# Half or all of a state-space layer's output product moved from VectorE to TensorE and ScalarE, in the units that have no expert tile

## The chip, the cores and the metric

The kernel runs on one NeuronCore of one Trainium2 chip. The metric is the time of one execution on the device in microseconds (us). Several executions are timed and their median is taken; one further execution is recorded by the hardware profiler.

## What is computed

A batch of 2 sequences of 2048 tokens with 128 features goes through a pre-norm block: a Mamba layer, a gated feed-forward layer, and a mixture of 8 experts of which every token uses 2. The change touches the Mamba layer's recurrence. Cut to that:

```python
x_dbl = xc @ x_proj_w.T
dt, Bm, Cm = jnp.split(x_dbl, [DT_RANK, DT_RANK + D_STATE], axis=-1)      # 16 states
delta = jax.nn.softplus(dt @ dt_w.T + dt_b)
dA  = jnp.exp(jnp.einsum('bld,dn->bldn', delta, -jnp.exp(A_log)))
dBu = jnp.einsum('bld,bln,bld->bldn', delta, Bm, xc)
def step(h, inp):
    dA_t, dBu_t, C_t = inp
    h = dA_t * h + dBu_t                          # the scan over tokens
    y = jnp.einsum('bdn,bn->bd', h, C_t)          # multiply by C, sum over the 16 states
    return (h, y)
y = (ys + xc * D) * jax.nn.silu(z)
return y @ out_w.T                                # then feed-forward, routing, experts
```

## The kernel before

The 4096 tokens are cut into 8 chunks of 512. The recurrence of a chunk is done in 16 *units*, one for each state n. A unit handles 256 inner channels (two halves of 128 partitions) by 512 tokens. A unit takes these steps, named as in the code:

- `fetch_b`, `fetch_c`: SyncE starts DMAs that spread one row of B and one row of C over 128 partitions (`b_wide`, `c_wide`).
- `inflow` (GpSimd, L670): `du` times `b_wide`, 128x1024.
- `decay` (ScalarE, L775): two exponentials of 128x512, one for each half, into two PSUM banks. The one for unit i+1 waits for the scan of unit i on the same half.
- `scan` (VectorE, L908): two scans of 128x512 into `state`, which has two slots. Scan i waits for `inflow` i, `decay` i and the release of its slot.
- `carry` (ScalarE, L779): saves the last column for the next chunk.
- `times_c` (VectorE, L916): `state` times `c_wide`, one product of 128x1024 into `product`, two slots.
- `total` (TensorE, L1104): eight 128x128 transposes of `product`, which add up in the PSUM banks `y0` and `y1` over the 16 units of the chunk.
- After unit 15 of a chunk `y_gate` (VectorE, L924) reads `y0` and `y1`. It stands in VectorE's order after the scan of unit 0 of the next chunk.

Between these steps stands other work, placed by the function `plan()`: in unit n of chunk c one row of the table `FRONT` (norm, convolution, projections, softplus of chunk c+1) and one row of `BACK` (output projection, feed-forward and routing of chunk c-1). From chunk 3 on, most units also hold one expert tile of 128 rows (`x_turn`, `gate`, `up`, `moe_h`, `down`, `y_rows`), which uses the PSUM banks `gate` and `up`. All engines walk the same list `order`, each taking its own steps, so that a waiting step holds up all that stands behind it on its engine. The units hold 38 of the 78 expert tiles; the other 40 come after the last unit ("the tail").

Steps of `FRONT` and `BACK` that matter below: at n=4 `conv1` and `tanh_c`; at n=5 `xc` (VectorE, L879) and `x_proj` (TensorE, L1068); at n=6 `n_turn`, `n_t`, `ff_gate` (L1134) and `x_dbl`; at n=7 `gate_h` (ScalarE, L802 and L803) and `ff_val` (L1137); at n=8 `ff_out` (L1140, L1142); at n=9 `x_four` (VectorE, L943) and `log_dt`, whose logarithm needs two loads of ScalarE's tables; at n=12 `m_turn` (L1038) and `route_mm` (L1151); at n=13 `z0` (L1087); at n=14 `rank` (L1158 to L1163) and `z1`.

## Time and profile before

| | before |
|---|---|
| median of 3 runs | 914.85 us (913.28 to 917.78) |
| the profiled execution, its own time | 916.48 us |
| its span in the trace | 914.6 us |
| mean granted TensorE clock | 0.789 of 2.4 GHz |
| busy: VectorE, TensorE, GpSimd, ScalarE | 84%, 69%, 63%, 49% of the span |

The profile is of one execution. Its own time is 1.9 us longer than its span and 1.6 us above the median. PE is TensorE, DVE is VectorE, ACT is ScalarE, POOL is GpSimd, and L908 is line 908 of the kernel before.

### The profile page before, as it was taken

Reading aid. Unit: us, or ns where it says so; the run is one execution under the profiler, and the core shown is the slowest. Engines: PE = TensorE matmul, PEld = TensorE weight load, DVE = VectorE, ACT = ScalarE, POOL = GpSimd, SP = SyncE. Lnnn points to the kernel's source line nnn. Section 1 sums busy time; section 2 is a strip of 40 time slices with the busy share of each in tenths; the row PEclk is TensorE's granted clock in tenths of the full one; section 3 lists DMA queues with packets and bytes.
Section 4 is the critical chain, followed back from the end, with each engine's and each line's share of the span. In section 5 each row is a group of like instructions: output and inputs, shape, how many; then the busy total and the mean of one; then the engine's idle time right before and its main releaser. Section 6 shows DMA issues by size and latency. Waiting matters only on the chain.

```text
span 914.6 us, 12461 instructions
## 1 busy us (share of the span) xinstructions
PE 634.4 (69%) x3482; PEld 488.9 (53%) x3482; DVE 766.2 (84%) x1158; ACT 447.8 (49%) x924; POOL 577.8 (63%) x488
## 2 busy tenths in 40 slices
PE   4357377478757785797589658865884686887874
PEld 1134354365346435684477337743773475777863
DVE  1389899999989989989999999999999996363453
ACT  2446455644654475545555564647553352333421
POOL 1096376458746995789668976898589845235422
PEclk9577578758656966997699768977796679799987
DMA  6734233333323346533553355335543553446694
GB/s 175 244 104 142 91 116 100 120 94 121 124 76 96 118 117 169 161 113 99 175 161 107 96 185 151 127 93 161 172 120 113 149 145 94 125 140 191 185 308 132
DMA packets 99767, 126.06 MB, mean 138 GB/s; under 512 B 11831, under 2 KB 63875, under 8 KB 99683
## 3 DMA queue, kind: packets, MB, share of 16 engines
q1 hardware_dynamic: 95155, 115.89, 42.7%
q0 software_dynamic: 4544, 9.38, 2.8%
q8 instruction: 29, 0.48, 0.2%
q14 instruction: 39, 0.32, 0.1%
HBM read 113.23 MB, written 16.34 MB: 142 GB/s over the span
## 4 chain that ended last, share of the span: by engine, by line
DVE 35%; PE 29%; issue 18%; ACT 7%; DMA 4%; SPq 3%; POOL 3%; DVEq 1%; another core or an unknown queue 0%; POOLq 0%; ACTq 0%
DVE state L908 19%; DVE product L916 4%; PE work_front L1062 4%; PE y L1104 3%; PE gate L1181 3%; PE work_front L1068 3%; PE up L1188 3%; PE up L1199 2%; DVE stats L841 2%; PE work_front L1076 1%; DVE silu_m L1027 1%; PE work_side L1142 1%; DMA y_dram<-y_rows,x_rows 1%; DVE x_tok L945 1%; DVE conv L882 1%
## 5 line engine op out<-in xcount | busy, mean ns | idle before, releaser
L670 POOL TENSOR_TENSOR inflow<-du,b_wide 128x1024 f32<-128x1024 f32 x128 | 308.9, 2416 | 191.6 <-DVE product L916 153.8
L775 ACT ACTIVATE decay<-delta,a_neg 128x512 f32<-128x512 f32 x256 | 174.0, 689 | 199.4 <-DVE state L908 191.5
L1104 PE MATMUL y<-ident,product 128*128 128x128 f32 x1024 | 181.8, 337 | 119.9 <-DVE product L916 119.9
L1104 PEld LDWEIGHTS y<-ident,product 128*128 128x128 f32 x1024 | 153.5, 177 | 172.9 <-DVE product L916 138.3
L908 DVE TENSOR_TENSOR_SCAN state<-decay,carry,inflow 128x512 f32<-128x512 f32 x192 | 235.2, 1266 | 0.8 <-ACT decay L775 0.8
L916 DVE TENSOR_TENSOR product<-state,c_wide 128x1024 f32<-128x1024 f32 x128 | 189.5, 1480 | 1.3
L697 POOL DMA_INDIRECT y_dram<-y_rows,x_rows x78 | 87.5, 1121 | 90.5 <-ACT y_rows L831 82.4
L691 POOL DMA_INDIRECT row_dram<-m_tok,place x64 | 71.8, 1122 | 22.1 <-issue 12.8
L908 DVE TENSOR_TENSOR_SCAN state<-decay,inflow 128x512 f32<-128x512 f32 x64 | 74.5, 1205 | 7.0 <-ACT decay L775 4.5
L1062 PE MATMUL work_front<-u_t,w_tap 128*128 128x512 f32 x128 | 63.0, 618 | 4.0 <-ACT u_t L725 1.7
L1181 PE MATMUL gate<-x_cols,w_stage 128*128 128x128 f32 x306 | 50.5, 309 | 7.4 <-ACT x_cols L821 6.9
L1199 PE MATMUL up<-w_down,h_cols 128*128 (+1 forms) x306 | 47.9, 296 | 8.8 <-DVE h_cols L1032 5.4
L1188 PE MATMUL up<-x_cols,w_stage 128*128 128x128 f32 x306 | 49.6, 304 | 5.3 <-ACT y_rows L831 3.3
L1181 PEld LDWEIGHTS gate<-x_cols,w_stage 128*128 128x128 f32 x306 | 44.5, 218 | 10.3 <-ACT x_cols L821 9.5
L1199 PEld LDWEIGHTS up<-w_down,h_cols 128*128 128x128 f32 (+1 forms) x306 | 41.1, 204 | 14.0 <-issue 14.0
L1188 PEld LDWEIGHTS up<-x_cols,w_stage 128*128 128x128 f32 x306 | 43.8, 216 | 6.3 <-ACT y_rows L831 4.1
L1068 PE MATMUL work_front<-xc,w_xproj 128*40 128x512 f32 x32 | 26.5, 978 | 27.5 <-DVE xc L879 27.5
L831 ACT ACTIVATE y_rows<-up,x_rows 128x128 f32<-128x128 f32 x51 | 18.7, 368 | 45.0 <-PE up L1199 37.6
L826 ACT ACTIVATE tanh_m<-gate 128x384 f32<-128x384 f32 x51 | 25.1, 492 | 30.7 <-PE gate L1181 23.4
L1087 PE MATMUL work_front<-w_in,u_t 128*128 128x256 f32 x64 | 24.2, 517 | 18.5 <-DVE silu_z L899 17.7
L1062 PEld LDWEIGHTS work_front<-u_t,w_tap 128*128 128x128 f32 x128 | 22.9, 198 | 24.8 <-issue 17.7
L1027 DVE SCALAR_TENSOR_TENSOR silu_m<-tanh_m,gate 128x384 f32<-128x384 f32 x51 | 27.4, 536 | 9.9 <-ACT tanh_m L826 7.1
(199 smaller groups left out, 1118.4 us busy)
## 6 DMA issues: line engine op xcount, KB each, us to landing
b_wide<-bc_dram SPq DMA_DIRECT2D x128, 256.0 KB
c_wide<-bc_dram SPq DMA_DIRECT2D x128, 256.0 KB
w_stage<-gate_up_dram SPq DMA_DIRECT2D x78, 344.0 KB
x_rows<-row_dram SPq DMA_DIRECT2D x78, 65.0 KB
x_tok<-in_x SPq DMA_DIRECT2D x8, 256.0 KB, 6.0
out<-x_tok SPq DMA_DIRECT2D x8, 256.0 KB
inflow<-y_dram SPq DMA_DIRECT2D x6, 256.0 KB, 4.8
gate_up_dram<-in_Wg SPq DMA_DIRECT2D x1, 1376.0 KB, 9.1
```

What stands on the lines that cost most here:

```text
L670: e.tensor_tensor(inflow[:, key % 3], du[:, c % 2], b_wide[:, key % ROW_SLOTS:key % ROW_SLOTS + 1, :].to_broadcast([P, HALVES, CHUNK]), AL ...
L691: e.indirect_dma_start(row_dram, bass.IndirectOffsetOnAxis(place[:, c, q, s:s + 1], 0), m_tok[:, c % M_SLOTS, s, :], None).then_inc(S[f"d_ ...
L697: e.indirect_dma_start(y_dram, bass.IndirectOffsetOnAxis(x_rows[:, key % X_SLOTS, ID_AT:ROW].bitcast(u32), 0), y_rows[:, key % Y_SLOTS, :] ...
L775: e.activation(decay_bank[h][:], delta[:, c % 2, h, :], ACT.Exp, scale=a_neg[:, h, n:n + 1]).then_inc(S["decay"], 1)
L908: e.tensor_tensor_scan(state[:, key % STATE_SLOTS, h, :], decay_bank[h][:], inflow[:, key % 3, h, :], 0.0 if c % (SEQ // CHUNK) == 0 else ...
L916: e.tensor_tensor(product[:, key % 2], state[:, key % STATE_SLOTS], c_wide[:, key % ROW_SLOTS:key % ROW_SLOTS + 1, :].to_broadcast([P, HAL ...
L1062: t = e.matmul(front[:], w_tap[:, k, h * P:(h + 1) * P], u_t[:, key % 2, k:k + CHUNK], start=k == 0, stop=k == D_CONV - 1)
L1068: t = e.matmul(front[0:BC + DT_RANK, :], w_xproj[:, h, :], xc[:, key % 2, h, :], start=h == 0, stop=h == HALVES - 1)
L1104: t = e.matmul(y_bank[s // 2][:, y_at(s, h)], product[:, key % 2, h, s * P:(s + 1) * P], ident[:], is_transpose=True, start=False, stop=n ...
L1181: t = e.matmul(gate[:, q * P:(q + 1) * P], w_stage[:, key % W_SLOTS, 0, q * P:(q + 1) * P], x_cols[:, key % 2, :], start=True, stop=True)
L1188: t = e.matmul(up[:, q * P:(q + 1) * P], w_stage[:, key % W_SLOTS, 1, q * P:(q + 1) * P], x_cols[:, key % 2, :], start=True, stop=True)
L1199: t = e.matmul(up[:, FF_WIDE:], h_cols[:n, key % 2, q, :], w_down[:n, bass.ds(experts[j % PICKS], 1), q, :].rearrange("p o d -> p (o d)"), ...
```

## The change

In units that have no expert tile (`free` in `plan()`, 46 of 128) C is applied by another way. The state itself is turned by TensorE into the idle banks `gate` and `up` (`h_turn`), so that tokens lie on partitions. There C is one number for each partition, and ScalarE copies the bank to SBUF with C as its scale (`c_scale`, into `h_rows`, one slot). TensorE then adds it to `y0` and `y1` by a product with the identity (`total`). In n=10 to 15 all four blocks of 128 tokens go this way, and VectorE's product and its C row are left out: 23 *full* units (six in each of chunks 0, 1 and 2, and n=10 in chunks 3 to 7). In n=4, 5 and 6 two of the four blocks do, and VectorE's product is 128x2x256: 23 *half* units (n=4 of chunk 4 is not among them). C turned for this is made once a chunk by four small products (`c_turn`) and one copy (`c_rows`). `inflow`, `scan` and `x_turn` get the waits that the new readers ask for, and `z0` now waits for `c_rows`. In the diff, `c_scale` is on ScalarE, `times_c` on VectorE, `total` and `h_turn` on TensorE.

```diff
+SHARES = {4: 2, 5: 2, 6: 2, 10: SUB, 11: SUB, 12: SUB, 13: SUB, 14: SUB, 15: SUB}
...
             turn(m, i)
+        if i in shares:
+            put("h_turn", i)
+            put("c_scale", i)
         put_all(back[1], front[1])
...
+        if not moving and ("x_turn", m) not in done and n in SHARES:
+            free.append(i)
         put("times_c", i)
...
+                elif name == "c_scale":
+                    c, n = UNITS[key]
+                    e.wait_ge(S["h_turn"], turned[key])
+                    e.wait_ge(S["y_sum"], key)
+                    e.wait_ge(S["c_rows"], c + 1)
+                    for sub in range(SUB - share[key], SUB):
+                        e.activation(h_rows[:, sub, :], h_bank[sub // 2][:, sub % 2 * D_INNER:(sub % 2 + 1) * D_INNER], ACT.Copy,
+                                     scale=c_tok[:, c % 2, sub, n:n + 1]).then_inc(S["c_scaled"], 1)
...
                 elif name == "times_c":
-                    c, n = UNITS[key]
+                    if share[key] == SUB:
+                        continue
+                    wide = (SUB - share[key]) * P
...
-                    e.tensor_tensor(product[:, key % 2], state[:, key % STATE_SLOTS],
-                                    c_wide[:, key % ROW_SLOTS:key % ROW_SLOTS + 1, :].to_broadcast([P, HALVES, CHUNK]), ALU.mult).then_inc(S["times_c"], 1)
+                    e.tensor_tensor(product[:, key % 2, :, :wide], state[:, key % STATE_SLOTS, :, :wide],
+                                    c_wide[:, key % ROW_SLOTS:key % ROW_SLOTS + 1, :wide].to_broadcast([P, HALVES, wide]), ALU.mult).then_inc(S["times_c"], 1)
...
                 elif name == "total":
-                    e.wait_ge(S["times_c"], key + 1)
-                    for s in range(SUB):
+                    alone = SUB - share[key]
+                    if alone:
+                        e.wait_ge(S["times_c"], products[key])
+                    for s in range(alone):
                         for h in range(HALVES):
                             t = e.matmul(y_bank[s // 2][:, y_at(s, h)], product[:, key % 2, h, s * P:(s + 1) * P], ident[:],
                                          is_transpose=True, start=False, stop=n == D_STATE - 1, skip_group_check=True)
+                    if share[key]:
+                        e.wait_ge(S["c_scaled"], scaled[key])
+                    for r in range(alone // 2, 2):
+                        t = e.matmul(y_bank[r][:], ident[:], h_rows[:, 2 * r:2 * r + 2, :].rearrange("p s d -> p (s d)"), start=False, stop=n == D_STATE - 1,
+                                     skip_group_check=True)
                     t.then_inc(S["y_sum"], 1)
+                elif name == "h_turn":
+                    e.wait_ge(S["scan"], HALVES * (key + 1))
+                    if scaled[key] > share[key]:
+                        e.wait_ge(S["c_scaled"], scaled[key] - share[key])
+                    if tiles_ahead[key]:
+                        e.wait_ge(S["y_rows"], tiles_ahead[key])
+                    for s in range(SUB - share[key], SUB):
+                        for h in range(HALVES):
+                            t = e.transpose(h_bank[s // 2][:, y_at(s, h)], state[:, key % STATE_SLOTS, h, s * P:(s + 1) * P], ident[:])
+                    t.then_inc(S["h_turn"], 1)
```

TensorE's order from the `total` of n=11 to that of n=14 in chunk 2. Before (`y<-ident,product` at L1104 is a `total`):

```order
L1104 MATMUL y<-ident,product 128x128 x32
L1038 MATMUL work_side<-ident,m_tok 128x128 x4
L1151 MATMUL work_side<-w_route,n_t 128x8 x4
L1104 MATMUL y<-ident,product 128x128 x8
L1087 MATMUL work_front<-w_in,u_t 128x256 x2
L1104 MATMUL y<-ident,product 128x128 x8
```

And of the change, from the `total` of n=11 to that of n=13 (L1172 is `h_turn`, L1156 the product of the identity with `h_rows` in `total`):

```order
L1156 MATMUL y<-h_rows,ident 128x512 x2
L1083 MATMUL work_side<-ident,m_tok 128x128 x4
L1172 MATMUL gate<-ident,state 128x128 x4
L1172 MATMUL up<-ident,state 128x128 x4
L1218 MATMUL work_side<-w_route,n_t 128x8 x4
L1156 MATMUL y<-h_rows,ident 128x512 x2
L1172 MATMUL gate<-ident,state 128x128 x4
L1172 MATMUL up<-ident,state 128x128 x4
L1132 MATMUL work_front<-w_in,u_t 128x256 x2
L1156 MATMUL y<-h_rows,ident 128x512 x2
```

In a full unit TensorE now has two steps in place of one, and the `total` of a unit stands ahead of the `h_turn` of the next.

TensorE's order from `x_proj` at n=5 to the `total` of n=6 in chunk 2, before:

```order
L1068 MATMUL work_front<-xc,w_xproj 40x512 x2
L1104 MATMUL y<-ident,product 128x128 x8
L1038 MATMUL work_side<-ident,m_tok 128x128 x4
L1134 MATMUL work_side<-n_t,w_ffg 128x512
L1076 MATMUL work_front<-x_dbl,w_dt 128x512
L1104 MATMUL y<-ident,product 128x128 x8
```

And of the change:

```order
L1113 MATMUL work_front<-xc,w_xproj 40x512 x2
L1151 MATMUL y<-ident,product 128x128 x4
L1156 MATMUL y<-h_rows,ident 128x512
L1083 MATMUL work_side<-ident,m_tok 128x128 x4
L1172 MATMUL up<-ident,state 128x128 x4
L1201 MATMUL work_side<-n_t,w_ffg 128x512
L1121 MATMUL work_front<-x_dbl,w_dt 128x512
L1151 MATMUL y<-ident,product 128x128 x4
L1156 MATMUL y<-h_rows,ident 128x512
```

The `h_turn` of n=6 now stands between `n_turn` (L1083) and `ff_gate` (L1201). On ScalarE the `c_scale` of the same unit now stands ahead of `n_t` (L837), for which `ff_gate` waits:

```order
L815 ACTIVATE decay<-delta,a_neg 128x512 x2
L819 ACTIVATE carry<-state 128x2
L780 ACTIVATE h_rows<-up,c_tok 128x256 x2
L837 ACTIVATE n_t<-work_side,norm_gb 128x512
L768 ACTIVATE x_dbl<-work_front 40x512
```

Before, `n_t` followed `carry` directly.

## Rows read from the trace of the kernel before

**Rows 1.** The page: busy time and share of the span of each engine.
```profile
PE 634.4 (69%) x3482; PEld 488.9 (53%) x3482; DVE 766.2 (84%) x1158; ACT 447.8 (49%) x924; POOL 577.8 (63%) x488
```

**Rows 2.** The page: costliest groups; busy us, mean ns, idle before and its releaser.
```profile
L775 ACT ACTIVATE decay<-delta,a_neg 128x512 f32<-128x512 f32 x256 | 174.0, 689 | 199.4 <-DVE state L908 191.5
L1104 PE MATMUL y<-ident,product 128*128 128x128 f32 x1024 | 181.8, 337 | 119.9 <-DVE product L916 119.9
L916 DVE TENSOR_TENSOR product<-state,c_wide 128x1024 f32<-128x1024 f32 x128 | 189.5, 1480 | 1.3
```

**Rows 3.** Timeline, VectorE, chunk 0, n=10 to `y_gate`: start, us, instruction.
```profile
95.59 2.34 DVE L908 TENSOR_TENSOR_SCAN state<-decay,inflow 128x512 f32<-128x512 f32 x2 [4.31 <-ACT decay L775]
...
126.56 1.27 DVE L924 TENSOR_TENSOR y_gated<-silu_z,y 128x512 f32<-128x512 f32 x2
```

**Rows 4.** Timeline, VectorE, chunk 1, n=10 to `y_gate`.
```profile
171.24 2.46 DVE L908 TENSOR_TENSOR_SCAN state<-decay,carry,inflow 128x512 f32<-128x512 f32 x2 [0.84 <-ACT decay L775]
...
186.39 1.21 DVE L916 TENSOR_TENSOR product<-state,c_wide 128x1024 f32<-128x1024 f32 x1
187.52 2.45 DVE L908 TENSOR_TENSOR_SCAN state<-decay,carry,inflow 128x512 f32<-128x512 f32 x2
...
207.57 1.26 DVE L924 TENSOR_TENSOR y_gated<-silu_z,y 128x512 f32<-128x512 f32 x2
```

**Rows 5.** Timeline, all engines: TensorE, ScalarE and VectorE at work like the new steps.
```profile
202.70 1.29 ACT L775 ACTIVATE decay<-delta,a_neg 128x512 f32<-128x512 f32 x2
203.47 0.68 DVE L899 SCALAR_TENSOR_TENSOR silu_z<-silu_z,work_front 128x512 f32<-128x512 f32 x1
207.02 1.11 PE L1038 MATMUL work_front<-ident,u_tok 128*128 128x128 f32 x4 [0.58 <-ACT u_tok L719]
208.41 0.76 ACT L725 ACTIVATE u_t<-work_front,norm_gb 128x512 f32<-128x512 f32 x1
213.41 1.04 PE L1104 MATMUL y<-ident,product 128*128 128x128 f32 x8
214.72 1.88 PE L1062 MATMUL work_front<-u_t,w_tap 128*128 128x512 f32 x4
229.74 1.97 PE L1104 MATMUL y<-ident,product 128*128 128x128 f32 x8 [3.23 <-DVE product L916]
234.43 3.54 PE L1068 MATMUL work_front<-xc,w_xproj 128*40 128x512 f32 x4 [2.73 <-DVE xc L879]
```

**Rows 6.** The groups by line, ScalarE: a copy with a scale, and one without.
```profile
L831 ACT ACTIVATE y_rows<-up,x_rows 128x128 f32<-128x128 f32 x51 | 18.7, 368 | 45.0 <-PE up L1199 37.6 <-remote 6.3 <-issue 1.1
...
L813 ACT ACTIVATE n_t<-work_side 128x512 f32<-128x512 f32 x8 | 4.7, 585 | 0.9 <-issue 0.9
```

**Rows 7.** Timeline, TensorE, the other steps of n=12 to 14 in chunk 1.
```profile
184.68 1.06 PE L1038 MATMUL work_side<-ident,m_tok 128*128 128x128 f32 x4
186.62 1.87 PE L1151 MATMUL work_side<-w_route,n_t 128*128 128x8 f32 x8 [0.88 <-ACT n_t L813]
...
196.68 0.63 PE L1158 MATMUL work_side<-both,before 128*128 128x32 f32 x2 [0.93 <-DVE both L980]
...
200.12 2.05 PE L1087 MATMUL work_front<-w_in,u_t 128*128 128x256 f32 x4
```

**Rows 8.** Windows: busy us of PE, PEld, DVE, ACT, POOL; granted clock, DMA.
```profile
95.00:127.00 32.00, 14.90 (x60) 11.95 (x60) 31.23 (x37) 14.96 (x33) 17.11 (x12) 0.55 0.25 81
171.00:208.00 37.00, 22.77 (x95) 18.96 (x93) 36.27 (x64) 16.83 (x39) 21.27 (x16) 0.55 0.29 92
258.00:295.00 37.00, 22.78 (x96) 19.55 (x96) 36.52 (x65) 15.82 (x36) 23.07 (x16) 0.55 0.29 92
127.00:171.00 44.00, 32.96 (x159) 20.00 (x158) 43.02 (x54) 28.89 (x49) 25.62 (x13) 0.89 0.38 128
```

**Rows 9.** Timelines, VectorE and TensorE: `x_four` at n=9 of chunks 3, 5; `ff_out`.
```profile
342.66 0.69 DVE L943 TENSOR_TENSOR x_two<-x_two,work_side 128x512 f32<-128x512 f32 x1 [3.25 <-PE work_side L1142]
...
532.62 0.67 DVE L943 TENSOR_TENSOR x_two<-x_two,work_side 128x512 f32<-128x512 f32 x1
...
530.45 1.16 PE L1142 MATMUL work_side<-w_ffp,gate_h 128*128 128x128 f32 x8
```

**Rows 10.** Timeline, VectorE and GpSimd: one product beside an `inflow`.
```profile
422.92 3.46 DVE L916 TENSOR_TENSOR product<-state,c_wide 128x1024 f32<-128x1024 f32 x1
422.92 2.37 POOL L670 TENSOR_TENSOR inflow<-du,b_wide 128x1024 f32<-128x1024 f32 x1
```

More of the change, by code:

```diff
@@ L76 @@
     ((), ("pre_dt1",), ("exp_dt",)),
-    (("log_dt",), (), ()),
-    ((), ("series", "small", "log1p"), ()),
+    (("log_dt",), (), ("c_turn",)),
+    ((), ("c_rows", "series", "small", "log1p"), ()),
     ((), ("delta",), ()),
@@ L113 @@
 HEAD = ["stats0", "rstd0", "rstd1", "shift0", "x_one", "prepare", "u_tok", "u_turn", "u_t", "halo", "in0a", "in0b", "conv0", "in1a", "in1b",
-        "conv1", "tanh_c", "xc", "x_proj", "x_dbl", "dt0", "pre_dt0", "dt1", "pre_dt1", "exp_dt", "log_dt", "series", "small", "log1p",
+        "conv1", "tanh_c", "xc", "x_proj", "x_dbl", "dt0", "pre_dt0", "dt1", "pre_dt1", "exp_dt", "log_dt", "c_turn", "c_rows", "series", "small", "log1p",
         "delta", "du"]
@@ L313, in plan @@
         put(step, last)
-    return order, tail
+    if not shares:
+        return plan(free)
+    return order, shares, tail
 def mamba_moe_block(nc, T, out):
@@ L445, in mamba_moe_block @@
             + ["dt", "pre_dt", "exp_dt", "log_dt", "ser0", "series", "small", "log1p", "delta", "du", "z", "tanh_z", "silu_z"]
-            + ["inflow", "decay", "scan", "carry", "times_c", "y_skip", "y_sum", "y_gate", "y_turn", "y_cols"]
+            + ["inflow", "decay", "scan", "carry", "times_c", "c_turn", "c_rows", "h_turn", "c_scaled", "y_skip", "y_sum", "y_gate", "y_turn", "y_cols"]
             + ["out_proj", "x_two", "n_tok", "n_turn", "n_t", "ff_gate", "gate_evac", "ff_val", "silu_g", "ff_h", "ff_out"]
@@ L668, in _ @@
                     if key >= 3:
-                        e.wait_ge(S["times_c"], key - 2)
+                        if share[key - 3] < SUB:
+                            e.wait_ge(S["times_c"], products[key - 3])
+                        else:
+                            e.wait_ge(S["scan"], HALVES * (key - 2))
                     e.tensor_tensor(inflow[:, key % 3], du[:, c % 2], b_wide[:, key % ROW_SLOTS:key % ROW_SLOTS + 1, :].to_broadcast([P, HALVES, CHUNK]),
@@ L1081, in _ @@
                     else:
[L1082 removed]
+                        e.wait_ge(S["c_rows"], key + 1)
                     if not key:
```

42 lines of the change are left out of this document (35 added, 7 removed).

## Prediction

> **What bounds the kernel now.** I read the page first. VectorE is busy for 84% of the span, TensorE for 69%, ScalarE for 49% [rows 1]. In the groups of the page the `decay` of ScalarE, the `total` of TensorE and, by its releaser column, most other work of the units wait for VectorE's scan or product, while the product itself hardly waits (1.3 us for 128) [rows 2]. So inside the units VectorE sets the pace, and a product of 1.2 us taken out of its queue should bring that much nearer the end, as long as nothing else becomes the last to arrive. That condition is the whole question, so I read VectorE's timeline next, in the three stretches where full units stand one behind the other: n=10 to 15 of chunks 0, 1 and 2. From the scan of n=10 to `y_gate`, the first instruction that needs the sums of all 16 units, 31.0 us pass in chunk 0 (95.59 to 126.56) [rows 3] and 36.3 us in chunk 1 (171.24 to 207.57) [rows 4]. In chunk 2, which repeats chunk 1, I take the same. VectorE is busy for 31.2 of 32 and 36.3 of 37 us there. TensorE has little to do and its granted clock is 0.55, so nearly all is at the lower level, 1.2 GHz. In the stretch between (127 to 171) it was 0.89 [rows 8]. A product takes a slot of 1.13 us in VectorE's order (186.39 to 187.52) [rows 4]. The last 40 expert tiles come after the units and the change does not touch them.
>
> **The new steps in a full unit.** No row shows them, so each is built from its nearest.
> - `h_turn`: eight 128x128 transposes, the same work as the old `total`: 1.04 us at the high clock, 1.97 at the low one [rows 5].
> - TensorE to ScalarE: the turn that ends at 208.13 releases `u_t` at 208.41, 0.28 us [rows 5].
> - `c_scale`: four copies of 128x256 from PSUM with a scale. A copy of 128x128 with a scale takes 0.368 [rows 6], a 128x512 with a scale 0.689 [rows 2], so 128x256 lies at 0.475. Two in a row overlap by 0.09 (2 x 0.689 less 1.29) [rows 5]. Four take 1.63 us.
> - `total`: two products of 128x512: 1.88 at the high clock, 3.54 at the low one [rows 5].
>
> These steps form a ring. `total` i waits for `c_scale` i, `c_scale` i for `h_turn` i, and `h_turn` i+1 stands behind `total` i on TensorE. There is one slot of `h_rows` and one pair of banks. So the ring cannot overlap with itself: a full unit cannot take less than 1.04 + 0.28 + 1.63 + 1.88 = **4.8 us** at the high clock and 1.97 + 0.28 + 1.63 + 3.54 = **7.4 us** at the low one. Behind a waiting `c_scale` on ScalarE stands the `decay` of unit i+2, and with it the scan, so VectorE is held to the ring after about one unit of lead. VectorE itself would need 36.3/6 less 1.13, about 4.9 us a unit in chunks 1 and 2, and 4.0 in chunk 0. The ring takes the product's place as the bound.
>
> Other steps of these units lie inside the ring in chunks 1 and 2, at the high clock (half the low-clock rows): `m_turn` 0.5; `m_t` and `route_mm`, which wait behind `c_scale` 12: 0.28 + 0.59 + 0.94 = 1.8 [rows 6, 7]; `rank` and `z1`, from 196.68 to 202.17 at the low clock, so 2.7, of which 1.9 lies beside `c_scale`: 0.8 [rows 7]. Sum 3.1 us; at the low clock 1.1 + 2.7 + 3.6 = 7.4.
>
> **Which clock.** The first full unit finds TensorE as idle as before: 7.4. In it TensorE works 5.5 of 7.4 us, more densely than before, and I expect the clock to rise during the second (6.1, the mean), and to stay up in the last four (4 x 4.8 = 19.2).
> - Chunk 0: 2.3 (scan) + 7.4 + 6.1 + 19.2 = 35.0 against 31.0: +4.0.
> - Chunks 1 and 2: 2.5 + 7.4 + 6.1 + 19.2 + 3.1 = 38.3 against 36.3: +2.0 each.
>
> Together **+8.0**. Bounds: all at the high clock, 31.1 and 34.4, so 0 and twice -1.9: -3.8. All at the low clock, 46.7 and 54.3, so +15.7 and twice +18.0: +51.7.
>
> The Trainium skill (TensorE: Matmul & The Clock Gate, Part 1) says that the low clock is the default and that activity releases it. By that rule alone, the added products would lift the clock in all of these stretches, and this term would be near its lower bound, -3.8. The trace agrees in direction (0.55 where TensorE is busy 15 of 32 us, 0.89 where it is busy 33 of 44) [rows 8], and not on whether a ring with gaps of 1.9 us is active enough.
>
> **Single full units** (n=10 of chunks 3 to 7). No second full unit follows, VectorE has three softplus steps there and ScalarE is free. The ring is hidden behind VectorE's n=10. The product's slot is gained: 5 x 1.13 = **-5.7**. If TensorE is late there, nothing is gained: 0.
>
> **Half units.** VectorE's half product is like a 128x512 (0.68 [rows 5] for 1.22): -0.54 each, -12.4 for all 23, if VectorE stays the last to arrive. A product that meets an `inflow` takes 3.46 us [rows 10], about one after the other; a half product meets it as well and saves no more. But at n=5 to 8 of chunks 1 to 7 there is a chain through TensorE: `xc`, `x_proj`, `total` 5, `n_turn`, `n_t`, `ff_gate`, `total` 6, `ff_val`, `ff_out`, `x_four`. In chunk 3 VectorE waits 3.25 us for its end [rows 9], and likewise in chunks 2, 4 and 7. Into this chain come, at the high clock: `total` 5 and `total` 6 each lose four transposes (0.52) and gain a product of 128x512 (0.94): +0.42 twice; `h_turn` 6: 0.52; `c_scale` 6 with its release, ahead of `n_t`: 0.28 + 0.86. Sum 2.5 (3.7 at the low clock). `xc` comes 0.5 earlier, which leaves +2.0 (3.2). So chunks 2, 3, 4 and 7: 4 x 2.0 = +8.0. In chunks 1, 5 and 6 VectorE doesn't wait, and comes about 1 us after the chain's end (531.6 against 532.6 in chunk 5) [rows 9]: 3 x 1.0 = +3.0. Chunk 0 has no such chain: 3 x -0.54 = -1.6. Sum **+9.4**. Bounds: -12.4 (the chain has room everywhere), and at the low clock 4 x 3.2 + 3 x 2.2 - 1.6 = +17.8.
>
> **The rest, at nothing.** `c_turn` and `c_rows`, once a chunk: four small products (like `route_mm`, 1.87 [rows 7]) and one copy of 128x64 (under 0.37 [rows 6]); they lie at n=9 and 10 beside VectorE's softplus steps, and `z0`, which waits for them, comes at n=13. Without that cover, 8 x 0.4 = 3 us on ScalarE. SyncE starts 23 C rows fewer; no B row is late now. ScalarE's own load, 138 copies of 0.41, fits into its idle half. The Trainium skill (ScalarE: Activation LUTs, Rules for kernel authors) advises VectorE for a multiplication. Here four copies take 1.63 us against one product of 1.22, so the move trades a shorter for a longer step and pays only where ScalarE is not in the chain.
>
> **Sum.** 8.0 + 9.4 - 5.7 = +11.7 us on the profiled execution's 916.5: 928.2. That execution is 1.6 above the median of 914.85, so **926.5 us** for the median.
>
> **The rivals.**
> - *The clock stays low in the rings.* For it: 0.55 now, and each `c_scale` leaves a gap. Against it: TensorE works for three quarters of a slow ring. All low gives 914.85 + 51.7 + 17.8 - 5.7 = 979; half of the way there from my value, about 953. Chance 0.15 for more than 940.
> - *The clock rises at once*, because the added products keep TensorE at work from the first full unit on. -3.8 + 9.4 - 5.7 = -0.1: 915, no difference. For it: 0.89 in the stretch in which TensorE has more work [rows 8]. Against it: the first full unit starts at the low clock. Chance 0.13. This is what the clock gate's rule of the Trainium skill, named above, would do here.
> - *VectorE stays the bound in the half units, so the kernel is faster.* Place: n=5 to 9. `h_turn` and `total` of n=4 and 5 give TensorE work just where it idles ahead of `x_proj`. If that keeps the clock up, `x_proj` alone takes 1.9 in place of 3.54 [rows 5], and two or three steps at the higher clock pay for the 2.0 us. It decides once the chain ends 2 us sooner in chunks 2, 3, 4 and 7. With the rings at the high clock: -3.8 - 12.4 - 5.7 = -21.9: 893; with my rings, 8.0 - 18.1 = -10.1: 905. For it: the chain ran at both clocks. Against it: `x_proj` would have to find the clock up although TensorE idles ahead of it, 2.73 us in chunk 2 [rows 5]. Chance 0.27.
> - *My forecast*, VectorE held by the rings and by the longer chain: 0.45, by itself 919.5 to 940.
>
> **How the numbers follow.** About 0.5% (4.6 us) is what a measurement of this kernel can tell from no change. Slower: 0.45 + 0.15 = 0.60. Within: 0.13. Faster: 0.27. The range leaves out about one in ten at each end: the best part of the faster case, below 900, and the worst part of the low clock, above 952.
>
> **What the profile after would show.** Right: in n=10 to 15 of chunks 0 to 2, the scans of VectorE are idle before, released by `decay`, and `decay` by `c_scale`; starts of `h_turn` 4.8 to 7.4 us apart; 35 and 38 us from the scan of n=10 to `y_gate`; longer waits of L988 (`x_four`) in chunks 2 and 3; four `c_scale` copies in 1.6 us. Wrong: scans back to back in these stretches; a granted clock near 1.0 there from the first full unit on; `x_four` without a wait. The forecast falls if one full unit's ring is much shorter than 4.8 us, or if the half units' chain ends before VectorE arrives.

## The result, and the profile after

| | before | changed |
|---|---|---|
| median | 918.35 us (913.28 to 927.35, 8 runs) | 907.12 us (905.76 to 913.85, 8 runs) |
| the profiled execution: its time, its span | 916.48, 914.6 us | 908.7, 906.5 us |
| mean granted TensorE clock | 0.789 | 0.870 |

The ratio is 0.990, with a 95% interval of 0.9861 to 0.9939: the changed kernel is faster by about 1%, some 9 us. Ratios and intervals here leave out executions more than 1.5% above the fastest of their kernel (before, the one at 927.35 us; of norings_late, the profiled one at 910.3 us), medians and ranges keep them. The forecast was slower, 926.5; the time lies in the range from 900 to 952, the sign was wrong.

The page of the changed kernel, busy line and groups (columns as in [rows 1, 2]):

```profile
PE 669.6 (74%) x3684; PEld 487.7 (54%) x3684; DVE 735.0 (81%) x1135; ACT 496.7 (55%) x1070; POOL 575.0 (63%) x488
...
L815 ACT ACTIVATE decay<-delta,a_neg 128x512 f32<-128x512 f32 x256 | 172.1, 690 | 113.6 <-DVE state L951 107.2
L961 DVE TENSOR_TENSOR product<-state,c_wide 128x1024 f32<-128x1024 f32 (+1 forms) x105 | 144.8, 1379 | 4.8 <-PE y L1151 3.4
...
L1156 PE MATMUL y<-h_rows,ident 128*128 128x512 f32 x138 | 90.2, 773 | 28.5 <-ACT h_rows L780 28.5
...
L780 ACT ACTIVATE h_rows<-up,c_tok 128x256 f32<-128x256 f32 x92 | 38.5, 474 | 14.8 <-PE up L1172 14.8
```

VectorE does 31 us less, and the kernel is 8 to 9 us shorter. So most of what VectorE was spared did not reach the end, and the questions are where it went and why anything was left. I looked at the three places that the prediction names.

**The full units of chunk 0**, TensorE's timeline of the changed kernel. L1172 is `h_turn`, L1156 `total`:

```profile
99.19 1.12 PE L1172 MATMUL gate<-ident,state 128*128 128x128 f32 x4 [5.23 <-DVE state L951]
100.10 1.06 PE L1172 MATMUL up<-ident,state 128*128 128x128 f32 x4
102.82 3.78 PE L1156 MATMUL y<-h_rows,ident 128*128 128x512 f32 x4 [1.66 <-ACT h_rows L780]
106.64 0.71 PE L1172 MATMUL gate<-ident,state 128*128 128x128 f32 x4
...
109.45 1.99 PE L1156 MATMUL y<-h_rows,ident 128*128 128x512 f32 x4 [1.66 <-ACT h_rows L780]
111.27 0.60 PE L1172 MATMUL gate<-ident,state 128*128 128x128 f32 x4
...
115.79 0.60 PE L1172 MATMUL gate<-ident,state 128*128 128x128 f32 x4
```

The ring is there. The first `h_turn` to the second takes 7.45 us at the low clock (predicted 7.4), from the second on 4.5 to 4.6 (predicted 6.1, then 4.8). In chunks 1 and 2, where other steps lie between, the starts are 7.6, 6.5, 5.9, 4.5 and 5.2 us apart, and 7.6, 5.0, 6.5, 5.4 and 5.2. Each wait of 1.66 us is four copies on ScalarE and the two hand-overs, of 0.03 to 0.06 us each. ScalarE's copies in the second ring of chunk 0, which begin when the turns end (107.79) and end 0.05 us before `total`:

```profile
107.83 0.84 ACT L780 ACTIVATE h_rows<-gate,c_tok 128x256 f32<-128x256 f32 x2 [0.39 <-PE up L1172]
108.56 0.84 ACT L780 ACTIVATE h_rows<-up,c_tok 128x256 f32<-128x256 f32 x2
```

Windows of the changed kernel (columns as in [rows 8]): the first ring of chunk 0, its other rings, n=10 to `y_gate` of chunks 1 and 2, and n=4 to 10 of chunks 2 and 3:

```profile
96.80:106.60 9.80, 5.75 (x12) 2.75 (x12) 9.66 (x8) 4.49 (x11) 3.15 (x1) 0.50 0.15 39
106.60:127.50 20.90, 14.31 (x65) 8.67 (x64) 16.40 (x23) 15.01 (x37) 15.90 (x11) 1.00 0.35 102
...
172.70:209.80 37.10, 26.24 (x109) 15.82 (x108) 31.81 (x58) 23.72 (x59) 24.13 (x18) 0.83 0.24 74
257.00:294.00 37.00, 26.54 (x108) 16.37 (x108) 33.90 (x57) 23.69 (x59) 23.74 (x18) 0.82 0.22 73
227.10:257.20 30.10, 22.15 (x99) 12.14 (x97) 28.11 (x33) 24.30 (x41) 20.90 (x12) 0.94 0.30 97
311.00:343.30 32.30, 22.24 (x88) 11.75 (x88) 31.44 (x34) 24.30 (x41) 27.29 (x27) 0.83 0.44 129
```

VectorE is now idle for 4.5 of 20.9 us in the rings, where it was busy for 31.2 of 32 [rows 8]. VectorE's timeline of the changed kernel gives the length of these stretches:

```profile
96.80 2.34 DVE L951 TENSOR_TENSOR_SCAN state<-decay,inflow 128x512 f32<-128x512 f32 x2 [4.32 <-ACT decay L815]
...
129.54 1.29 DVE L969 TENSOR_TENSOR y_gated<-silu_z,y 128x512 f32<-128x512 f32 x2 [2.93 <-PE y L1156]
...
172.74 2.46 DVE L951 TENSOR_TENSOR_SCAN state<-decay,carry,inflow 128x512 f32<-128x512 f32 x2 [1.54 <-ACT decay L815]
...
209.76 1.28 DVE L969 TENSOR_TENSOR y_gated<-silu_z,y 128x512 f32<-128x512 f32 x2 [1.03 <-PE y L1156]
```

Chunk 0: 32.7 us against 31.0 [rows 3] (predicted 35.0). Chunk 1: 37.0 against 36.3 [rows 4] (predicted 38.3). Chunk 2: 37.0 against 36.4. So the 18 products that left these stretches bought nothing: they became 3.0 us *longer*.

**The half units' chain**, chunk 2. First the kernel before, then the changed one: `xc`, `ff_out`, `x_four` (for `x_proj` before: [rows 5]).

```profile
233.17 1.21 DVE L879 SCALAR_TENSOR_TENSOR xc<-tanh_c,conv 128x1024 f32<-128x1024 f32 x1
...
252.42 2.08 PE L1142 MATMUL work_side<-w_ffp,gate_h 128*128 128x128 f32 x8
...
254.53 0.69 DVE L943 TENSOR_TENSOR x_two<-x_two,work_side 128x512 f32<-128x512 f32 x1 [3.46 <-PE work_side L1142]
```

```profile
234.19 1.21 DVE L919 SCALAR_TENSOR_TENSOR xc<-tanh_c,conv 128x1024 f32<-128x1024 f32 x1
...
235.45 1.91 PE L1113 MATMUL work_front<-xc,w_xproj 128*40 128x512 f32 x4 [1.68 <-DVE xc L919]
...
250.46 1.16 PE L1209 MATMUL work_side<-w_ffp,gate_h 128*128 128x128 f32 x8
...
251.69 0.66 DVE L988 TENSOR_TENSOR x_two<-x_two,work_side 128x512 f32<-128x512 f32 x1
```

From `xc` to `x_four` 21.4 us became 17.5, although TensorE has more to do between them. `x_proj` takes 1.91 in place of 3.54, `ff_out` 1.16 in place of 2.08, and `x_four` no longer waits. The granted clock of n=4 to 10 of this chunk is 0.94 [windows above], before it was 0.64. In chunk 3 `x_proj` still runs at the low clock (3.64 us), and the same distance falls all the same, from 21.0 to 17.9 us. The groups of `x_four`, of before and of the changed kernel, whose last columns are VectorE's idle time ahead of it:

```profile
L943 DVE TENSOR_TENSOR x_two<-x_two,work_side 128x512 f32<-128x512 f32 x8 | 5.4, 679 | 10.6 <-PE work_side L1142 10.6
```

```profile
L988 DVE TENSOR_TENSOR x_two<-x_two,work_side 128x512 f32<-128x512 f32 x8 | 5.3, 666 | 2.4 <-PE work_side L1209 2.4
```

The forecast had this wait grow by 2 us in each of four chunks. It shrank by 8.2 in all. The prediction also read it wrongly: it has a wait "likewise in chunks 2, 4 and 7", and before, these were 3.46, 0.81 and 0.66 us (3.25 in chunk 3). In chunks 4 and 7:

```profile
437.73 0.69 DVE L943 TENSOR_TENSOR x_two<-x_two,work_side 128x512 f32<-128x512 f32 x1 [0.81 <-PE work_side L1142]
...
721.72 0.69 DVE L943 TENSOR_TENSOR x_two<-x_two,work_side 128x512 f32<-128x512 f32 x1 [0.66 <-PE work_side L1142]
```

The remaining 2.38 us of both groups stand in the tail, behind the last unit, and stay.

**Something that the prediction did not have.** VectorE and GpSimd just behind the scan of n=10 in chunk 1, before:

```profile
174.93 0.69 DVE L886 TENSOR_SCALAR tanh_c<-tanh_c 128x1024 uint32<-128x1024 f32 x1
...
178.22 2.35 POOL L670 TENSOR_TENSOR inflow<-du,b_wide 128x1024 f32<-128x1024 f32 x1 [3.98 <-DVE product L916]
```

and in the changed kernel:

```profile
175.36 3.15 POOL L696 TENSOR_TENSOR inflow<-du,b_wide 128x1024 f32<-128x1024 f32 x1 [0.33 <-DVE state L951]
...
176.41 2.65 DVE L926 TENSOR_SCALAR tanh_c<-tanh_c 128x1024 uint32<-128x1024 f32 x1
```

Before, the `inflow` of n=13 waited for the product of n=10 (178.22). Now that there is no product, it waits for the scan (175.36), comes 3 us sooner, and meets the comparison of softplus (`small`). That takes 2.65 us in place of 0.69. Scan 10 to scan 11 grew from 6.7 to 7.6 us, although a product of 1.13 is gone. In chunks 3 to 6 GpSimd still has two steps of a norm (`rstd`) to do there, this `inflow` starts only after the comparison has ended (at 348.65 in chunk 3, where the comparison starts at 347.06 and takes 0.69), and the same distance shrank by 1.07 to 1.35 us (in chunk 3 from 6.83 to 5.76). In chunk 7, without softplus steps, it shrank by 1.26.

### The profile page after: what moved, and what is told of

It reads as the page before. It is cut to its first block, busy times and chain, and to the rows that moved or that the text cites. A ratio compares the mean times of both kernels' runs of the same rounds, so it can differ in the third digit from the quotient of the medians.

```text
span 906.5 us, 13029 instructions
## 1 busy us (share of the span) xinstructions
PE 669.6 (74%) x3684; PEld 487.7 (54%) x3684; DVE 735.0 (81%) x1135; ACT 496.7 (55%) x1070; POOL 575.0 (63%) x488
## 4 chain that ended last, share of the span: by engine, by line
PE 25%; DVE 20%; issue 12%; ACT 6%; DMA 2%; SPq 2%; another core or an unknown queue 1%; POOL 0%; DVEq 0%; ACTq 0%; POOLq 0%
DVE state L951 10%; PE gate L1250 3%; PE up L1268 2%; DVE product L961 2%; PE up L1257 2%; PE y L1156 2%; PE y L1151 2%; PE work_front L1107 2%; PE work_front L1113 1%; ACT decay L815 1%; DVE stats L881 1%; DVE silu_m L1072 1%; DVE x_tok L990 1%; PE decay L1250 1%
## 5 line engine op out<-in xcount | busy, mean ns | idle before, releaser
L696 POOL TENSOR_TENSOR inflow<-du,b_wide 128x1024 f32<-128x1024 f32 x128 | 317.3, 2482 | 177.5 <-DVE product L961 116.9
L815 ACT ACTIVATE decay<-delta,a_neg 128x512 f32<-128x512 f32 x256 | 172.1, 690 | 113.6 <-DVE state L951 107.2
L961 DVE TENSOR_TENSOR product<-state,c_wide 128x1024 f32<-128x1024 f32 (+1 forms) x105 | 144.8, 1379 | 4.8 <-PE y L1151 3.4
L1151 PE MATMUL y<-ident,product 128*128 128x128 f32 x748 | 111.7, 294 | 42.5 <-DVE product L961 42.5
L1151 PEld LDWEIGHTS y<-ident,product 128*128 128x128 f32 x748 | 91.9, 152 | 80.4 <-DVE product L961 50.1
L1156 PE MATMUL y<-h_rows,ident 128*128 128x512 f32 x138 | 90.2, 773 | 28.5 <-ACT h_rows L780 28.5
L717 POOL DMA_INDIRECT row_dram<-m_tok,place x64 | 72.6, 1134 | 24.6 <-issue 14.6
L1107 PE MATMUL work_front<-u_t,w_tap 128*128 128x512 f32 x128 | 65.7, 641 | 6.0 <-ACT u_t L751 4.4
L1156 PEld LDWEIGHTS y<-h_rows,ident 128*128 128x128 f32 x138 | 28.9, 239 | 51.6 <-ACT h_rows L780 35.5
L1257 PE MATMUL up<-x_cols,w_stage 128*128 128x128 f32 x306 | 47.6, 295 | 6.9 <-ACT y_rows L871 6.9
L780 ACT ACTIVATE h_rows<-up,c_tok 128x256 f32<-128x256 f32 x92 | 38.5, 474 | 14.8 <-PE up L1172 14.8
```

Source lines behind the costliest of these rows:

```text
L696: e.tensor_tensor(inflow[:, key % 3], du[:, c % 2], b_wide[:, key % ROW_SLOTS:key % ROW_SLOTS + 1, :].to_broadcast([P, HALVES, CHUNK]), AL ...
L717: e.indirect_dma_start(row_dram, bass.IndirectOffsetOnAxis(place[:, c, q, s:s + 1], 0), m_tok[:, c % M_SLOTS, s, :], None).then_inc(S[f"d_ ...
L815: e.activation(decay_bank[h][:], delta[:, c % 2, h, :], ACT.Exp, scale=a_neg[:, h, n:n + 1]).then_inc(S["decay"], 1)
L961: e.tensor_tensor(product[:, key % 2, :, :wide], state[:, key % STATE_SLOTS, :, :wide], c_wide[:, key % ROW_SLOTS:key % ROW_SLOTS + 1, :wi ...
L1107: t = e.matmul(front[:], w_tap[:, k, h * P:(h + 1) * P], u_t[:, key % 2, k:k + CHUNK], start=k == 0, stop=k == D_CONV - 1)
L1151: t = e.matmul(y_bank[s // 2][:, y_at(s, h)], product[:, key % 2, h, s * P:(s + 1) * P], ident[:], is_transpose=True, start=False, stop=n ...
```

## The experiments

One table for all: the ratio to the kernel before, run beside each on the same chip, and from the one profile of each three sums over VectorE's timeline, from the start of one scan to that of another: (a) n=10 to n=1 of the next chunk, chunks 0 to 2; (b) the same, chunks 3 to 6; (c) n=4 to n=10, all eight chunks, with the granted clock there.

| | median | ratio, 95% interval | a | b | c, clock |
|---|---|---|---|---|---|
| before | | | 111.8 | 170.7 | 258.8, 0.74 |
| copy | 916.15 | 0.9986 (0.9957 to 1.0015) | 111.7 | 173.1 | 256.1, 0.74 |
| changed kernel | 907.12 | 0.9900 (0.9861 to 0.9939) | 113.9 | 165.4 | 248.9, 0.89 |
| halves | 912.39 | 0.9931 (0.9903 to 0.9960) | 111.7 | 175.4 | 249.1, 0.88 |
| fulls | 908.34 | 0.9897 (0.9865 to 0.9929) | 113.4 | 165.6 | 249.8, 0.80 |
| warm | 912.11 | 0.9932 (0.9906 to 0.9958) | 111.7 | 172.5 | 250.0, 0.86 |
| half_product | 908.36 | 0.9890 (0.9841 to 0.9939) | 111.6 | 173.0 | 244.0, 0.76 |
| no_c | 896.44 | 0.9767 (0.9733 to 0.9801) | 100.9 | 166.9 | 251.1, 0.80 |
| two_slots | 906.71 | 0.9887 (0.9851 to 0.9923) | 109.8 | 169.0 | 247.2, 0.86 |
| norings | 904.13 | 0.9857 (0.9824 to 0.9891) | 113.8 | 166.8 | 246.1, 0.86 |
| late_inflow | 906.46 | 0.9897 (0.9861 to 0.9933) | 111.3 | 165.3 | 248.5, 0.88 |
| warm_ring | 909.80 | 0.9908 (0.9872 to 0.9944) | 114.3 | 165.4 | 248.2, 0.88 |
| singles | 905.16 | 0.9862 (0.9818 to 0.9906) | 111.7 | 165.5 | 247.3, 0.85 |
| norings_late | 897.77 | 0.9783 (0.9744 to 0.9822) | 107.9 | 169.5 | 251.2, 0.85 |

Column a repeats to 0.2 us where nothing of it was changed (before, copy, halves, warm, half_product, singles). Columns b and c differ by more between executions in which nothing of them was changed (b by 2.4 us in copy and 4.7 in halves, c by 2.7 in copy), and the clock of single chunks differs with them, so they carry a verdict only together with the timed ratio.

### copy: the kernel before, once more

No edit. 

> The kernel before once more, unchanged but for an empty line, as a second profile of it and as a measure of what no change looks like. All theories: a ratio of 1 within its interval. It tells how far the stages n=0 to 4, 4 to 10 and 10 to 16 of single profiled executions differ without any change: the profile before had 258.8 us in n=4 to 10 over all chunks, and each of the four edited kernels 244 to 250. If the copy has 250 as well, that difference was the draw of one execution and no effect of the half units.

Measured: 0.9986, no difference. Its column c is 256.1 us, so of the 9.9 us that this column is shorter in the changed kernel, some 3 can be the draw of one execution, and not all. `x_four` waits as before, 11.7 us.

### halves and fulls: one part of the change at a time

```diff
-SHARES = {4: 2, 5: 2, 6: 2, 10: SUB, 11: SUB, 12: SUB, 13: SUB, 14: SUB, 15: SUB}
+SHARES = {4: 2, 5: 2, 6: 2}                                    # halves
+SHARES = {n: SUB for n in range(10, D_STATE)}                  # fulls
```

> The change with the 23 half units only; no unit is full. Theory A (the half units give the gain, because TensorE's added work keeps its clock up in n=4 to 10 and the chain from xc to x_four ends sooner; the full units together are worth little): 907 to 911 us against about 917 before, the granted clock of n=4 to 10 in chunks 2, 3 and 7 up by 0.1 or more against 0.64, 0.70 and 0.60. Theory B (my prediction's term: the half units cost 9 us, and the gain is in the full ones): 924 to 928 us. Theory C (the gain is from the full units' clock, which carries over into the other stages): about 917, no difference.

> The change with the 23 full units only; no unit is half. Theory A: the rings of chunks 0 to 2 cost about 3 us, the five single units gain 5.5, so 913 to 917 us. Theory B: 905 or less. Theory C: 907 to 910.

Measured: the half units alone gain 6.3 us, the full ones alone 9.5, both together 9.2. The half units' term of the forecast (+9.4) thus has the wrong sign. The gains don't add: whatever each of them gives, they partly give the same. The profiled execution of halves, at 920.2 us, is the slowest of its twelve. That full units gain 9.5 is more than the single ones in column b (5.1) less the 1.6 that column a costs. The time of fulls lies in the range of Theory C (907 to 910), a clock that carries over into other stages. The rest appears in column c, where fulls adds only `c_turn` (1.06 us of TensorE once a chunk) but the granted clock of chunks 2 and 3 is 0.83 and 0.83 after 0.64 and 0.70. How much of it is chance, a single profile can't say, and no run shows what carries the clock over.

### warm: TensorE's added work without VectorE's saving

The kernel before, with one 128x512 product of constants into the idle bank `up` behind the `total` in each of the 23 half units. Nobody reads it.

```diff
                     t.then_inc(S["y_sum"], 1)
+                    if key in tiles:
+                        if tiles[key]:
+                            e.wait_ge(S["y_rows"], tiles[key])
+                        e.matmul(up_bank[:], ident[:], w_in[:], start=True, stop=True)
```

> The kernel before with one more product of 128x512 on TensorE in each of the 23 half units, right behind the unit's total, of constants into the idle bank up, read by nobody; VectorE and ScalarE as before. The output is the reference's. It has TensorE's load of the half units without VectorE's saving. Theory A (clock): the granted clock of n=4 to 10 rises as in the changed kernel and the kernel is faster than before by 3 to 8 us. Rival (VectorE's shorter product gives the gain, TensorE's work only costs): the same as before or slower by up to 5 us.

Measured: 0.9932, 6.2 us faster by work that serves nothing. The group of `x_four`:

```profile
L946 DVE TENSOR_TENSOR x_two<-x_two,work_side 128x512 f32<-128x512 f32 x8 | 5.4, 672 | 3.1 <-PE work_side L1149 3.1
```

VectorE waits 3.1 us there in place of 10.6, and the granted clock of n=4 to 10 is 0.86 in place of 0.74. That the clock is higher is not the draw of one profile: over its twelve executions the mean granted clock is 0.808 to 0.824, against 0.776 to 0.796 for the kernel before. VectorE's load is unchanged, so here the clock shortens the chain.

### half_product: VectorE's saving without the added work

```diff
+                    wide = 2 * P if key in tiles else CHUNK
-                    e.tensor_tensor(product[:, key % 2], state[:, key % STATE_SLOTS], ...
+                    e.tensor_tensor(product[:, key % 2, :, :wide], state[:, key % STATE_SLOTS, :, :wide], ...
```

> The kernel before with VectorE's product cut to 128x2x256 in the 23 half units; TensorE turns the same eight blocks as before, half of them old data. Left out: half of the multiplication by C in these units. It has VectorE's saving without any work for TensorE or ScalarE. Theory A (clock): at most 3 us faster, since the chain's end at x_four still comes late at the low clock in chunks 2, 3, 4 and 7. Rival (the shorter product gives the gain): 8 to 12 us faster.

Measured: 0.9890, 10.1 us for 23 half products of 0.54 each (12.4). By the interval it is 5.6 to 14.6 us. VectorE is the bound in most of these units: much of what it is spared arrives at the end, at a mean clock of 0.76 in column c, hardly above the old one. My chain, which should have swallowed this, holds only where VectorE waits for it, and that was 8.2 us in all units together. How much is VectorE's saving alone, the run doesn't show. In its profile the granted clock of chunks 2 and 3 is 0.76 and 0.80 after 0.64 and 0.70, without added work, and `x_four` waits there no longer (in chunk 4 it waits 3.70); column c is shorter by 14.8 us, more than the 12.4 of the products. halves has this saving, the warmth of TensorE and the new steps, and gains 6.3. If the three simply added, the new steps in the chain would cost about 10 us (10.1 + 6.2 - 6.3). That sum is arithmetic, no run isolates it.

### no_c: full units without their ring

fulls, but the turned state goes straight into `y`: no `c_scale`, no product with the identity, one `total` of eight transposes.

```diff
-            put("c_scale", i)
...
+                        for s in range(SUB):
+                            for h in range(HALVES):
+                                t = e.matmul(y_bank[s // 2][:, y_at(s, h)], state[:, key % STATE_SLOTS, h, s * P:(s + 1) * P], ident[:],
+                                             is_transpose=True, start=False, stop=n == D_STATE - 1, skip_group_check=True)
```

> Full units only, without the ring: in the 23 full units VectorE's product is left out and TensorE's total turns the state straight into the sum; no h_turn, no c_scale, no identity product. Left out: the multiplication by C in these units. It shows what the 23 products are worth on VectorE. If the rings of chunks 0 to 2 hold VectorE as I predicted (h_turn starts 4.5 us apart), this kernel is 12 to 20 us faster than the one with the full units only (about 908), so 890 to 897. If the rings hold nothing, it is within 4 us of it.

Measured: 0.9767, 21.4 us, against 9.5 for fulls. The difference of 11.9 us is in column a: 100.9 against 113.4. So the detour (the separate turn, the copies, the products with the identity) costs 12.5 us in 18 units, and takes all that their products release (10.9 here, where the comparison still takes 2.65 us and scan 10 to 11 7.4 to 7.6). In chunk 0 TensorE does denser work than before, without a 128x512 product. Its window there, scan 11 to the scan behind n=15:

```profile
104.30:122.10 17.80, 10.72 (x48) 8.55 (x48) 17.77 (x25) 8.94 (x19) 14.05 (x11) 0.63 0.25 82
```

### two_slots: a ring that may overlap with itself

```diff
-        h_rows = sb("h_rows", [P, SUB, D_INNER])
+        h_rows = sb("h_rows", [P, 2, SUB, D_INNER])
...
+            if late:                       # n = 11 to 15: total i-1 behind h_turn i
+                put("total", i - 1)
```

> The changed kernel with a second slot of h_rows, and in n=11 to 15 of chunks 0 to 2 the total of a unit put behind the h_turn of the next, so that the identity products of one unit lie beside the c_scale of the next. If the ring holds VectorE: the starts of h_turn fall from 4.5 us apart to 3.4 to 4, n=10 to y_gate from about 33 and 37 us to 27 and 31, and the kernel is 8 to 15 us faster than the changed one (about 909). If it is VectorE's and ScalarE's own order that holds these units: within 3 us of it.

Measured: 0.9887, hardly better than the changed kernel. TensorE's timeline shows that the ring is broken open in chunk 0:

```profile
99.06 1.12 PE L1175 MATMUL gate<-ident,state 128*128 128x128 f32 x4 [3.66 <-DVE state L954]
...
106.48 1.12 PE L1175 MATMUL gate<-ident,state 128*128 128x128 f32 x4 [5.45 <-DVE state L954]
...
111.38 0.60 PE L1175 MATMUL gate<-ident,state 128*128 128x128 f32 x4
...
114.17 0.63 PE L1175 MATMUL gate<-ident,state 128*128 128x128 f32 x4
```

From the third on the starts are 2.8 to 3.9 us apart in place of 4.5, and chunk 0 takes 30.1 us from n=10 to `y_gate` (32.7 in the changed kernel, 27 expected). But the second turn (106.48) now waits for the scan, no longer for the ring, and still comes 7.4 us after the first: it is scan 11 that is late, behind softplus and its collision. In chunks 1 and 2, 38.5 and 38.8 us of column a (39.4 and 39.3 in the changed kernel) are left, so what the ring held there is 0.9 us and less a chunk, and other steps of n=11 to 15 come next.

### norings: full units without a neighbour

`SHARES = {4: 2, 5: 2, 6: 2, 10: SUB}`: n=10 stays full in all chunks, n=11 to 15 go back to VectorE. 

> The changed kernel without full units in n=11 to 15: half units, and n=10 full in all eight chunks. My theory now (a ring costs about what it saves, 1 to 2 us a chunk): within 4 us of the changed kernel, 905 to 912. Rival (the 15 full units behind n=10 carry the gain, by the clock that they keep up): slower than the changed kernel by 5 to 9 us.

Measured: 0.9857. That is within 4 us of the changed kernel, as expected, at 904.1 just below the expected 905. Column a is 113.8, that of the changed kernel. The 15 full units behind n=10 in chunks 0 to 2 are worth nothing: they trade their products for waits on the ring.

### late_inflow and norings_late: the collision taken away

```diff
                             e.wait_ge(S["scan"], HALVES * (key - 2))
+                    if n == 13 and c < 3:
+                        e.wait_ge(S["small"], c + 2)
```

> The changed kernel, with one wait more: in chunks 0 to 2 the inflow of n=13, which GpSimd computes, starts only after VectorE's softplus comparison (small, 128x1024). In the changed kernel this inflow waits for the scan of n=10 in place of a product, runs beside the comparison, and the comparison takes 2.65 us in place of 0.69. Theory H (this collision cancels the gain of n=10 in these chunks): the comparison takes 0.7 again, scan 10 to scan 11 falls from 7.4 to 7.6 us to about 5.7, and the kernel gains up to 3 x 1.9 = 5.7 us on the changed one: ratio to the kernel before 0.982 to 0.986, some 902 to 904. Theory R (the rings from n=10 on hold the stretch in any case): scan 10 to 11 falls, but the waits behind it grow by as much, n=10 to y_gate stays at 32.7 and 37.0 us within 0.5, and the time stays at 906 to 908, ratio 0.988 to 0.991.

> Half units, and n=10 full in all chunks, none behind it; and in chunks 0 to 2 the inflow of n=13 starts only after the softplus comparison, as in late_inflow. No ring can take back what the comparison gains. If the collision (2.65 us for 0.69) is what eats the gain of n=10 there, scan 10 to scan 11 of chunks 0 to 2 is about 5.7 us and the kernel is some 3 to 5 us faster than the one with n=10 full and no late inflow (0.9857): ratio 0.980 to 0.983, 900 to 902. If that inflow was hidden and something else is next in line, the ratio stays at 0.984 to 0.987.

GpSimd and VectorE of norings_late in chunk 1:

```profile
177.55 0.69 DVE L928 TENSOR_SCALAR tanh_c<-tanh_c 128x1024 uint32<-128x1024 f32 x1
...
178.41 3.38 POOL L698 TENSOR_TENSOR inflow<-du,b_wide 128x1024 f32<-128x1024 f32 x1 [2.24 <-DVE tanh_c L928]
```

The comparison takes 0.69 us again, and scan 10 to 11 is 5.6 (173.87 to 179.50). Without rings behind it this goes to the end: column a falls by 5.9, three times 2.0, and the median by 6.4 (904.13 to 897.77; ratio 0.9857 to 0.9783), more than expected. This is the best of all kernels here that compute the whole result. Of its profile only column a is used. With the rings, the same edit does nothing: 0.9897 against 0.9900, and n=10 to `y_gate` is 32.3, 36.4 and 35.5 us against 32.7, 37.0 and 37.0. The ring takes back most of it, as Theory R has it, if not all in chunk 2 (1.5 us shorter, against the 0.5 that it allows).

### singles: full units only where they are alone and meet nothing

`SHARES = {4: 2, 5: 2, 6: 2, 10: SUB}`, and in chunks 0 to 2 no full unit. 

> Half units as in the changed kernel, and full units only for n=10 of chunks 3 to 7 (5 in place of 23). No ring follows another anywhere, and chunks 0 to 2 have no full unit, so inflow doesn't meet the softplus comparison. If rings and the collision in chunks 0 to 2 together cost what the product brings or more (chunk 0 +1.7, chunks 1 and 2 +0.7 by the one profile), this is faster than the changed kernel: chunk 0 to 2 as before, about -2 to -3 us on the changed one: 904 to 905, ratio 0.983 to 0.987. If the full units there bring a gain by the clock that they leave behind, it is slower than the changed kernel: above 909, ratio over 0.991.

Measured: 0.9862, column a as before, column b 165.5. Five full units in place of 23 give at least as much as the change does.

### warm_ring: TensorE kept at work ahead of the first ring

```diff
+        if n == 10 and c < 3:
+            put("warm", i)                 # two 128x512 products of constants into up
```

> The changed kernel, with two 128x512 products of constants into the idle bank of up, in front of the turn of n=10 in chunks 0 to 2 (ahead of the scan of n=10 in the order; nobody reads them). They keep TensorE at work where it idles 5.23 us before the first turn of chunk 0. Theory L (the first ring is long because it starts at the low clock): the interval from the first to the second h_turn of chunk 0 falls from 7.45 to about 4.6 us, and n=10 to y_gate of chunk 0 from 32.7 by 1 to 3 us; chunks 1 and 2, whose first total ran at the high clock already, stay; the time is 904 to 907, ratio 0.985 to 0.989. Theory V (VectorE's softplus steps between scan 10 and scan 11 hold the first unit, not the ring): the interval may fall, but n=10 to y_gate stays within 0.5 us, and the ratio at 0.988 to 0.991.

Measured: 0.9908, no gain, and neither expectation met. Windows of its chunk 0: ahead of the products, with them, and the first ring.

```profile
88.00:96.00 8.00, 6.91 (x33) 5.47 (x33) 6.43 (x6) 7.00 (x9) 5.50 (x3) 0.70 0.43 143
96.00:101.00 5.00, 3.07 (x7) 1.20 (x5) 2.18 (x2) 4.09 (x6) 1.02 (x1) 0.79 0.25 54
101.00:108.00 7.00, 5.13 (x12) 2.55 (x12) 6.86 (x6) 2.88 (x8) 3.15 (x1) 0.53 0.11 37
```

The products ran (TensorE busy 3.07 of 5 us, clock 0.79), and the ring behind them still had 0.53. The clock rose for good one ring later than in the changed kernel, and n=10 to `y_gate` took 34.4 us (32.7). In chunk 1 the same products did what they were put in for: the turn of n=10 ran at the high clock, the first ring took 6.31 us in place of 7.60, and the stretch 35.5 in place of 37.0. Chunk 2 took 37.2 (37.0). Work put a few microseconds ahead of a ring thus helped in one of three chunks; what sets the moment stays open.

## Why the prediction was right or wrong

**The rings: mechanism right, size off.** The starts of `h_turn` (7.45 and 4.5 to 4.6), the first ring at the low clock, four `c_scale` copies (1.6 us) and VectorE's idle time are as forecast. The term was +8.0, and the same stretches measure +3.0 (1.7 + 0.7 + 0.6). Two pieces are mis-sized. The ring at the high clock, put at 4.8, takes 4.52, mostly because the hand-overs, put at 0.28, are 0.03 and 0.05. Over five rings that is 1.4 us, about as much as the 1.3 by which each of chunks 1 and 2 is shorter than forecast; the last four rings of chunk 0 are 0.9 shorter by it. And "the second 6.1, the mean" took 4.63 in chunk 0, where the clock rose as the second ring began (106.80). In chunk 1 the second ring ran half at the low clock, as forecast, and took 6.5 with `m_turn` in it. The 3.1 us of other steps there were not too much: the five rings behind the first took 26.9 us, 4.0 more than in chunk 0. And for the first full unit the limit was not the ring alone. two_slots shows scan 11 late by itself, and late_inflow and norings_late show that 2.0 us of this are the collision, which the working doesn't have. It was there to be foreseen. The diff moves `inflow` from `times_c` to `scan`, and [rows 10] show a product of 1.2 us at 3.46 beside an `inflow`. I had asked what the product's absence does for VectorE, and not what it releases on GpSimd. The Trainium skill (SBUF — State Buffer, Who interferes with whom) says that VectorE and GpSimd share a pair of ports, that a `tensor_scalar` can need it, and that whichever starts first has it for its whole instruction. The trace agrees: the comparison ends 0.6 us after the `inflow` (2.65 for 0.69), and in norings_late, where `inflow` starts beside a running instruction of VectorE, it is `inflow` that is longer (3.38 for 2.35). The small steps that the prediction put at nothing were small: `c_turn` 1.06 us of TensorE, `c_rows` 0.24 of ScalarE.

**The single full units: right.** -5.7 for five was forecast; scan 10 to 11 of chunks 3 to 7 fell by 1.07 to 1.35, together 5.9, and column b, with four of the five, by 5.3.

**The half units: wrong, and this turned the sign.** The step was "into this chain come, at the high clock: ... sum 2.5" on top of an unchanged clock, and with it "chunks 2, 3, 4 and 7: 4 x 2.0 = +8.0". halves measures -6.3 for a forecast of +9.4. Two parts of the step fail. First, the chain ran at a higher clock, 0.89 after 0.74 in these stretches, and its 2.5 us of new steps are more than paid by the old steps at the high clock (in chunk 2 `x_proj` and `ff_out`). warm shows that added work alone raises the clock and brings 6.2 us. It isn't the only thing that can: in the profiles of fulls and half_product, which add none or next to none here, the clock of chunks 2 and 3 rose as well. Secondly, I let the chain decide in chunks 4 and 7, where VectorE waited 0.81 and 0.66 us for it, as in chunks 2 and 3, and in chunks 1, 5 and 6, where VectorE comes after it, and so gave away VectorE's saving everywhere (half_product gains 10.1 us, for 12.4 of products). The rival "VectorE stays the bound in the half units", with my rings 905, comes nearest to what happened. Its condition, that the chain ends 2 us sooner, was met in chunks 2 and 3 (21.4 to 17.5, and 21.0 to 17.9). That its 905 is so near to the measured 907 is in part luck: it has the rings 5 us too dear and the half units 6 us too good. The argument held against it, that `x_proj` would have to find the clock up although TensorE idles ahead of it, was wrong in chunk 2: it idles for 1.68 us there and `x_proj` takes 1.91. In chunk 3 `x_proj` did run at the low clock, and the chain was shorter all the same. That activity releases the low clock, which the Trainium skill says (TensorE: Matmul & The Clock Gate, Part 1) and the prediction names for the rings, pointed the right way here, and I had not applied it to the half units.

**The sum.** Between the profiled spans (-8.1): column a +2.1, b -5.3, c -9.9, together -13.1. The other +5.0 lie outside these columns, where the change does little but the -1.3 of the single full unit of chunk 7. n=0 to 4 of chunk 0 alone has +2.9, at a granted clock of 0.64 after 0.78 (two_slots and singles, with the same steps there, have none of it), and copy shows +3.9 in n=0 to 4 of all chunks. The measured parts, halves -6.3, the rings +3.0 and the single units -5.9, do add up to the measured 9.2. But by the same parts fulls alone would gain 2.9, and it gains 9.5, so this agreement proves nothing.

**What stays open.** Why fulls gains 9.5 us, how much the half units' new steps cost by themselves, and what decides the moment at which the clock rises.

## What to carry to other kernels

Where a helper engine idles between short bursts, the work that is moved to it can change its clock, and with it every step that is already there: cost the old chain at both clocks before giving the new steps a price. When an instruction is taken out, list all that waited for it, on every engine: what comes free sooner can meet something that it never met, and one wait put back (`inflow` behind `small`) can be worth much of the whole change (from 0.9857 to 0.9783, where the change brought 0.9900). A detour in three steps over two engines with one slot paid here once, beside other work; six in a row only traded one bound for another.
